# Attention inner loop on Trainium2: weighting V one key tile later, with three slots for the exponentials

## Chip, cores, metric

One Trainium2 chip, one program on all 8 of its cores. Each core takes one of the 8 batch elements (4096 tokens of width 1024) and does the whole computation for it; no data goes between cores. The metric is the device time in microseconds (us) of the slowest core.

## What is computed

For each batch element the reference does an attention block and a gated feed-forward block, each between two LayerNorms and with a residual. Cut to what matters:

```python
def attn(latents, gamma, beta, Wq, Wk, Wv, Wo):          # 16 heads of 64
    x = layernorm(latents) * gamma + beta
    q, k, v = x @ Wq, x @ Wk, x @ Wv                     # split into heads
    scores  = einsum('bhqd,bhkd->bhqk', q * s, k * s)    # s*s = 1/8
    weights = softmax(scores, axis=-1)
    return einsum('bhqk,bhkd->bhqd', weights, v) @ Wo
x = x + layernorm(attn(layernorm(x), ...))
x = x + layernorm(ffn(layernorm(x), ...))                # token shift, sigmoid gate, relu^2
```

## The kernel before

The kernel is written by hand, engine by engine. `ph.op(engine, ...)` (L34) puts an instruction at the end of one engine's list, `ph.wait` (L41) puts a wait on a semaphore there, and every engine works through its list in order. So what order things happen in is the order in which the Python code emits them, and the waits are those that are written out.

Stages: LayerNorm of the input and a bf16 copy to HBM; projections of Q, K and V (L356, L509); attention (L750 to L949) with the output projection and its LayerNorm for the query chunk before woven in; then the feed-forward stage (from L976). The change touches only the attention stage.

**Attention.** There are 8 chunks of 512 queries (`qc`), and in each 8 pairs of heads (`pj`), so 64 rounds (`idx`), here called heads' rounds, or rounds for short. A round goes over the 4096 keys in 32 key tiles of 128 (`kt`). One key tile is:

- *scores* (L782, TensorE): two matmuls, one for each head of the pair, 64 rows each, that run side by side on the array and write 128 keys x 512 queries each into `ps_sc`. `ps_sc` has four PSUM banks, so two key tiles' scores: the bank pair is `kt % 2`. Scores of tile `kt` wait for the exponential of `kt-2`, which empties that pair.
- *exponential* (L858, ScalarE): one ACTIVATE over both heads, 128x1024, from `ps_sc` to `exp_sb` in bf16. A fixed bound takes the place of the row maximum, so nothing is rescaled. `exp_sb` has two slots of 1024 columns, also by `kt % 2`.
- *weighting V* (L848, TensorE): two matmuls, one for each head, that add 65 x 512 into `ps_o[0]` and `ps_o[1]` over all key tiles. Row 65 comes from a column of ones in `v_sb` and is the sum of the exponentials.

TensorE's order is: scores of `kt`, then V of `kt-1`, which waits for the exponential of `kt-1`. The last tile's V matmuls (the *tail*, L871) are emitted in the next round, behind its first scores.

**End of a round.** VectorE waits for the tail (`s_mm2`), copies `ps_o` to `stage` (L885, two copies) and takes the reciprocal of the sums (L903, two of 1x512). The first V matmul of the next round waits for the two copies (`s_aev`), since it overwrites `ps_o`. In the next round, behind the scores of key tile 8, TensorE spreads the reciprocals over 64 rows (the *broadcast*, L914, four fp32 matmuls on `ps_bcj`, waiting for `s_rec`), VectorE multiplies (L923) into `attnb`, and the SyncE queue writes `attnb` to HBM (L930). In the last round of a chunk (`pj` = 7) ScalarE makes the reciprocals instead (L892, L897) and tail and broadcast stand at once at the end of the round.

**Woven in.** At key tile 8 of `pj` = 1, 3, 5 of every chunk but the first, TensorE also does 16 matmuls of the output projection (L629), between whose two halves it waits for a copy by VectorE (L637). ScalarE and VectorE do small LayerNorm steps at key tile 8 of the rounds.

Of the kernel before, what the change touches and what calls it, by code (L numbers as in the profile page):

```python
# [8 lines left out]
BF16 = mybir.dt.bfloat16  # L9
# [44 lines left out]
def build_nc(S=4096, D=1024, H=16, dh=64):  # L54
# [25 lines left out]
    with ExitStack() as top:  # L80
# [21 lines left out]
        d_attn = sem2("d_attn")  # L102
# [12 lines left out]
        s_exp = sem("s_exp")  # L115
        s_mm2 = sem("s_mm2")
# [11 lines left out]
        P = perm.enter_context  # L128
# [6 lines left out]
        stage_sb = [P(nc.sbuf_tensor(f"stage{i}", [128, 512], F32)) for i in range(4)]  # L135
        attnb_sb = [P(nc.sbuf_tensor(f"attnb{i}", [64, 512], BF16)) for i in range(4)]
        qm_sb = P(nc.sbuf_tensor("qm_sb", [1, 2 * NP * QC], F32))
# [17 lines left out]
        ph = Emit()  # L155
# [13 lines left out]
        Pc = p2core.enter_context  # L169
        kT_sb = Pc(nc.sbuf_tensor("kT_sb", [128, NP * S], BF16))  # L170
        exp_sb = Pc(nc.sbuf_tensor("exp_sb", [128, 2048], BF16))
        qtc_sb = Pc(nc.sbuf_tensor("qtc_sb", [128, NP * 512], BF16))
        ps_sc = Pc(nc.psum_tensor("ps_sc", [128, 2048], F32))
        ps_o = [Pc(nc.psum_tensor(f"ps_o{i}", [128, 512], F32)) for i in range(2)]
        ps_bcj = Pc(nc.psum_tensor("ps_bcj", [128, 512], F32))
        ps_bc = [ps_bcj[0:64, :], ps_bcj[64:128, :]]
# [67 lines left out]
        for i in range(NT):  # L244
# [31 lines left out]
            if i >= 2:  # L276
# [3 lines left out]
                  inc=s_s)  # L280
# [52 lines left out]
        for ch in range(QC):  # L333
# [14 lines left out]
            for (wsb, is_q) in ((wq_sb, True), (wk_sb, False)):  # L348
                for o in range(NP):
# [42 lines left out]
        for j2 in range(2 * NP):  # L392
# [15 lines left out]
              inc=s_v)  # L408
# [341 lines left out]
        for qc in range(QC):  # L750
# [8 lines left out]
            for pj in range(NP):  # L759
# [5 lines left out]
                for kt in range(KT):  # L765
# [25 lines left out]
                    if kt == min(8, KT - 1):  # L791
# [6 lines left out]
                        if qc >= 1:  # L798
# [23 lines left out]
                            else:  # L822
# [9 lines left out]
                                else:  # L832
# [4 lines left out]
                                    if pj < NP - 1:  # L837
                                        p3a_stepT(t0 + pj)
                    if kt >= 1:
                        if kt == 1 and idx >= 1:  # L840
                            ph.wait("tensor", s_aev, ps_o_free_chk[idx - 1])
                        ph.wait("tensor", s_exp, chk_kt[kt - 1])
                        bpo = ((kt - 1) % 2) * 2
                        for r2 in range(2):
                            hh = 2 * pj + r2
                            ph.op("tensor", lambda e, kt=kt, hh=hh, r2=r2, bpo=bpo,
                                  st=(kt == 1):
                                  e.matmul(ps_o[r2][0:65, :],  # L848
                                           v_sb[:, (kt - 1) * HW + hh * 65: (kt - 1) * HW + hh * 65 + 65],
                                           exp_sb[:, (bpo + r2) * 512:(bpo + r2 + 1) * 512],  # L850
                                           start=st, stop=False))
                    ph.wait("scalar", s_sct, sct_chk)
                    if kt == 0:
                        ph.wait("scalar", s_v, bias_ready)
                    if kt == 1 and idx >= 1:
                        ph.wait("scalar", s_mm2, 2 * idx)
                    ph.op("scalar", lambda e, bp=bp, pj=pj:
                          e.activation(exp_sb[:, bp * 512:(bp + 2) * 512],  # L858
                                       ps_sc[:, bp * 512:(bp + 2) * 512],
# [3 lines left out]

                def mk_tail(chk31=chk_kt[KT - 1], pj=pj):
                    def emit():
                        ph.wait("tensor", s_exp, chk31)
                        bpo = ((KT - 1) % 2) * 2
                        for r2 in range(2):
                            hh = 2 * pj + r2
                            ph.op("tensor", lambda e, hh=hh, r2=r2, bpo=bpo:  # L870
                                  e.matmul(ps_o[r2][0:65, :],  # L871
                                           v_sb[:, (KT - 1) * HW + hh * 65: (KT - 1) * HW + hh * 65 + 65],
                                           exp_sb[:, (bpo + r2) * 512:(bpo + r2 + 1) * 512],
                                           start=False, stop=True),
                                  inc=s_mm2)
                    return emit
# [55 lines left out]
                attn_w_chk[idx] = d_attn[pi].n
# [341 lines left out]
```

How the kernel before makes its waits and increments, by code:

```python
    def op(self, eng, fn, inc=None, k=1):  # L31
        if inc is not None:
            self.q[eng].append(lambda e, fn=fn, s=inc.h, k=k: fn(e).then_inc(s, k))
            inc.n += k
        else:
            self.q[eng].append(fn)
# [1 line left out]
    def wait(self, eng, sem, val=None):  # L38
        v = sem.n if val is None else val
        if v > 0:
            self.q[eng].append(lambda e, s=sem.h, v=v: e.wait_ge(s, v))
```

## Time and profile before

| what | us |
|---|---|
| median of 2 runs | 4059.81 (4054.91 to 4064.7) |
| the profiled execution, its own time | 4071.57 |
| span of its slowest core (core 2) | 4069.8 |
| spans of the eight cores | 4040.3 to 4069.8 |
| attention stage on core 2 (first exponential to last) | 691 to 3343 |

The profile shows one execution. The span goes from the first instruction to the last of a core. Instruction times are in us, or in ns where marked so. Idle time is put down to whatever released the engine. A pair of instructions of one line that overlap or touch is merged into one row of the timeline, with its count.

### The profile page before, as it was taken

How to read it: one execution, taken by the hardware profiler on the slowest of the kernel's cores; microseconds unless marked ns; L12 is line 12 of the kernel's file. 1: busy time of each engine (PE TensorE's matmuls, PEld its weight loads, DVE VectorE, ACT ScalarE, POOL GpSimd, SP SyncE). 2: the span in 40 equal slices, each digit the busy share in tenths (PEclk: the TensorE clock that was granted, in tenths of full speed). 3: DMA queues.
4: the chain of work that ended last, by engine and by line, in shares of the span. 5: the costliest groups of instructions: out<-in, count | busy, mean ns of one | idle time of the engine just before them, and what ended most of it. 6: DMA issues, size and time to landing. Idle time of an engine off the chain costs nothing.

```text
span 4069.8 us, 40105 instructions; the slowest of 8 cores (4040.3 to 4069.8 us)
## 1 busy us (share of the span) xinstructions
PE 2900.7 (71%) x12324; PEld 883.4 (22%) x12324; DVE 1411.9 (35%) x1953; ACT 2489.3 (61%) x2675; POOL 107.7 (3%) x201
## 2 busy tenths in 40 slices
PE   0477759777777777777778777777777772476675
PEld 0133323221222222222122222222212210232232
DVE  3466653212232232223233223322313223445444
ACT  3300001888888788788887878878888870232433
POOL 1011000000000000000000000000000001000000
PEclk9999979999999999999999999999999996777888
DMA  7521123000000100100101010010010005243241
GB/s 180 149 50 47 42 44 81 3 10 20 14 21 20 37 28 16 34 23 21 38 16 30 11 37 28 16 41 16 28 32 18 23 24 118 49 95 61 57 99 62
DMA packets 173284, 176.73 MB, mean 43 GB/s; under 512 B 112656, under 2 KB 137232, under 8 KB 173088
## 3 DMA queue, kind: packets, MB, share of 16 engines
q1 hardware_dynamic: 145792, 100.71, 10.5%
q0 software_dynamic: 22688, 65.07, 6.1%
q10 hardware_dynamic: 4608, 8.39, 0.6%
q8 instruction: 116, 1.90, 0.2%
q14 instruction: 80, 0.66, 0.1%
HBM read 96.49 MB, written 67.14 MB: 40 GB/s over the span
## 4 chain that ended last, share of the span: by engine, by line
PE 44%; ACT 31%; issue 9%; DVE 8%; DMA 3%; SPq 2%; DVEq 2%; ACTq 1%; POOL 0%; POOLq 0%
ACT exp_sb L858 28%; PE ps_o L848 15%; PE ps_sc L782 9%; PE ps_sc L356 6%; PE ps_sc L509 3%; PE ps_w L629 2%; PE ps_k L1130 2%; PE ps_wo L1104 2%; DVEq L44 2%; SPq L1045 2%; PE ps_bcj L914 2%; DVE sq_sb L311 1%; DMA wk_sb<-wk 1%; DVE xrT_sb L1076 1%; DVE xkT_sb L1082 1%
## 5 line engine op out<-in xcount | busy, mean ns | idle before, releaser
L858 ACT ACTIVATE exp_sb<-ps_sc,bias_cols 128x1024 bf16<-128x1024 f32 x2048 | 2181.6, 1111 | 580.5 <-PE ps_sc L782 579.1
L848 PE MATMUL ps_o<-exp_sb,v_sb 128*65 128x512 bf16 x3968 | 1198.3, 383 | 492.4 <-ACT exp_sb L858 414.3
L782 PE MATMUL ps_sc<-qtc_sb,kT_sb 64*128 64x512 bf16 x4096 | 808.6, 392 | 1.1 <-DVE v_sb L519 1.1
L885 DVE COPY stage<-ps_o 65x512 f32<-65x512 f32 x128 | 82.2, 681 | 1595.2 <-PE ps_o L871 1595.2
L848 PEld LDWEIGHTS ps_o<-exp_sb,v_sb 128*65 128x65 bf16 x3968 | 282.3, 109 | 1048.1 <-issue 1043.4
L782 PEld LDWEIGHTS ps_sc<-qtc_sb,kT_sb 64*128 64x128 bf16 x4096 | 196.0, 93 | 859.0 <-issue 859.0
L903 DVE RECIPROCAL stage<-stage 1x512 f32<-1x512 f32 x112 | 367.1, 3315 | 5.1
L1104 PE MATMUL ps_wo<-wrt_sb,xrT_sb 128*128 128x512 bf16 x512 | 138.9, 437 | 132.0 <-DVE xkT_sb L1085 80.9
L402 ACT ACTIVATE nmag_sb<-prod_sb 1x8 f32<-1x8 f32 x1 | 0.2, 207 | 369.9 <-DVE prod_sb L398 369.9
L1164 PE MATMUL ps_wo<-wvt_sb,kact_sb 128*128 128x512 bf16 x512 | 137.4, 433 | 111.2 <-DVE gg_sb L1185 98.3
L629 PE MATMUL ps_w<-wo_sb,at_sb 128*128 128x512 bf16 x512 | 141.2, 425 | 77.5 <-DVE wo_sb L637 67.4
L356 PE MATMUL ps_sc<-xat_sb,wq_sb 128*128 128x512 bf16 x512 | 121.8, 399 | 82.4 <-DMA xat_sb<-xa_h 82.4
L923 DVE TENSOR_TENSOR attnb<-stage,ps_bcj 64x512 bf16<-64x512 f32 x128 | 87.6, 684 | 192.9 <-PE ps_bcj L914 190.9
L356 PE MATMUL ps_sc<-xat_sb,wk_sb 128*128 128x512 bf16 x512 | 123.4, 403 | 0.0
L1130 PE MATMUL ps_k<-xkT_sb,wkt_sb 128*128 128x512 bf16 x512 | 119.1, 397 | 0.0
L509 PE MATMUL ps_sc<-wv_sb,xat_sb 128*128 128x512 bf16 x512 | 113.4, 385 | 4.3 <-DVE wv_sb L483 4.3
L1104 PEld LDWEIGHTS ps_wo<-wrt_sb,xrT_sb 128*128 128x128 bf16 x512 | 54.3, 109 | 216.9 <-issue 183.9
L1197 ACT ACT_TABLE_LOAD x8 | 10.3, 1283 | 148.4 <-DVE mv L1194 148.4
L914 PE MATMUL ps_bcj<-stage,ones128f 1*64 1x512 f32 x256 | 73.2, 648 | 33.2 <-ACT stage L897 33.2
L1164 PEld LDWEIGHTS ps_wo<-wvt_sb,kact_sb 128*128 128x128 bf16 x512 | 53.9, 108 | 194.8 <-issue 160.9
L1145 DVE TENSOR_TENSOR kact_sb<-k_sb 128x512 bf16<-128x512 bf16 x64 | 27.2, 426 | 185.8 <-ACT k_sb L1140 185.8
L629 PEld LDWEIGHTS ps_w<-wo_sb,at_sb 128*128 128x128 bf16 x512 | 49.6, 105 | 177.6 <-issue 140.5
(117 smaller groups left out, 1656.5 us busy)
## 6 DMA issues: line engine op xcount, KB each, us to landing
x_sb<-x SPq DMA_DIRECT2D x64, 512.0 KB, 5.1
x_h<-x1r_sb POOLq DMA_DIRECT2D x32, 512.0 KB, 2.9
x1c_sb<-x_h POOLq DMA_DIRECT2D x8, 2048.0 KB, 18.9
out<-ob_sb SPq DMA_DIRECT2D x8, 2048.0 KB, 12.6
xa_h<-xa_sb ACTq DMA_DIRECT2D x32, 256.0 KB, 4.7
qt_h<-qstage POOLq DMA_DIRECT2D x64, 128.0 KB, 2.2
qtc_sb<-qt_h SPq DMA_DIRECT2D x16, 512.0 KB, 4.8
attn_h<-attnb SPq DMA_DIRECT2D x128, 64.0 KB, 2.2
```

What stands on the lines that cost most here:

```text
L356: e.matmul(ps_sc[:, b * 512:(b + 1) * 512], w[:, c * D + o * 128: c * D + o * 128 + 128], xat_sb[:, (pxt * CT + c) * 512:(pxt * CT + c + 1 ...
L509: e.matmul(ps_sc[:, b * 512:(b + 1) * 512], xat_sb[:, (pxt * CT + c) * 512 + it * 128: (pxt * CT + c) * 512 + it * 128 + 128], wv_sb[:, c ...
L629: e.matmul(ps_w3[:], at3_sb[:, c * 512 + it * 128: c * 512 + it * 128 + 128], wo_sb[:, c * D + ec * 512: c * D + ec * 512 + 512], start=st ...
L782: e.matmul(ps_sc[:, (bp + r2) * 512:(bp + r2 + 1) * 512], kT_sb[lo:lo + 64, pj * S + kt * 128: pj * S + (kt + 1) * 128], qtc_sb[lo:lo + 64 ...
L848: e.matmul(ps_o[r2][0:65, :], v_sb[:, (kt - 1) * HW + hh * 65: (kt - 1) * HW + hh * 65 + 65], exp_sb[:, (bpo + r2) * 512:(bpo + r2 + 1) * ...
L858: e.activation(exp_sb[:, bp * 512:(bp + 2) * 512], ps_sc[:, bp * 512:(bp + 2) * 512], AF.Exp, bias=bias_cols[:, pj:pj + 1], scale=0.125),
L903: e.reciprocal(stage_sb[si][64:65, :], stage_sb[si][64:65, :]),
L914: e.matmul(ps_bc[r2], ones128f[64:65, :], stage_sb[si][64:65, :], start=True, stop=True, tile_position=(64, 64 * r2)), inc=s_bct)
L923: e.tensor_tensor(attnb_sb[si][:], stage_sb[si][0:64, :], ps_bc[r2], ALU.mult), inc=s_amu)
L1104: e.matmul(ps_wo[ppw][:, ec * 512:(ec + 1) * 512], xrT_sb[:, (pp * CT + c) * 512 + it * 128: (pp * CT + c) * 512 + it * 128 + 128], wrt_sb ...
L1130: e.matmul(ps_k3[ppk][:], wkt_sb[:, c * D + o * 128: c * D + o * 128 + 128], xkT_sb[:, (pp * CT + c) * 512:(pp * CT + c + 1) * 512], start ...
L1164: e.matmul(ps_wo[ppw][:, ec * 512:(ec + 1) * 512], kact_sb[:, c * 512 + it * 128: c * 512 + it * 128 + 128], wvt_sb[:, c * D + ec * 512: c ...
```

## The change

V is weighted two key tiles behind the scores, where it was one. Four things go with that. `exp_sb` gets a third slot, by `kt % 3`. The tail holds the V matmuls of the last two key tiles, 30 and 31. The first V matmul of a round, with its wait for VectorE's copies, now stands behind the scores of key tile 2, where it was tile 1. The first exponential of a round gets a wait of its own: for the V matmuls of key tile 30, which read the slot that it writes. `attnb` goes from four buffers to two, so the wait for its write to HBM moves from ahead of the copies to ahead of the multiply, and is for the write of one round before, where it was two.

```diff
-        attnb_sb = [P(nc.sbuf_tensor(f"attnb{i}", [64, 512], BF16)) for i in range(4)]
+        attnb_sb = [P(nc.sbuf_tensor(f"attnb{i}", [64, 512], BF16)) for i in range(2)]
...
-        exp_sb = Pc(nc.sbuf_tensor("exp_sb", [128, 2048], BF16))
+        exp_sb = Pc(nc.sbuf_tensor("exp_sb", [128, 3072], BF16))
...
-                    if kt >= 1:
-                        if kt == 1 and idx >= 1:
+                    if kt >= 2:
+                        ktg = kt - 2
+                        if kt == 2 and idx >= 1:
                             ph.wait("tensor", s_aev, ps_o_free_chk[idx - 1])
-                        ph.wait("tensor", s_exp, chk_kt[kt - 1])
-                        bpo = ((kt - 1) % 2) * 2
+                        eo = (ktg % 3) * 1024
...
                     if kt == 0:
                         ph.wait("scalar", s_v, bias_ready)
+                        if idx >= 1:
+                            ph.wait("scalar", s_mm2, 2 * idx - 1)
                     if kt == 1 and idx >= 1:
                         ph.wait("scalar", s_mm2, 2 * idx)
...
-                        ph.wait("tensor", s_exp, chk31)
...
+                        for ktg in (KT - 2, KT - 1):
+                            ph.wait("tensor", s_exp, chk30 if ktg == KT - 2 else chk31)
+                            eo = (ktg % 3) * 1024
...
+                                      inc=(s_mm2 if r2 == 1 else None))
...
-                if idx >= 2:
-                    ph.wait("vector", d_attn[pi], attn_w_chk[idx - 2])
...
                 ph.wait("vector", s_bct, 2 * (idx + 1))
+                if idx >= 1:
+                    ph.wait("vector", d_attn[(idx - 1) % 2], attn_w_chk[idx - 1])
```

**TensorE within a round.** The first rows of the attention stage. Before: scores of tiles 0 and 1 (L782), V of tile 0 (L848), scores of tile 2.

```order
L782 MATMUL ps_sc<-qtc_sb,kT_sb 128x512 [waits s_v,s_pjv,d_qtr0]
L782 MATMUL ps_sc<-qtc_sb,kT_sb 128x512 x3
L848 MATMUL ps_o<-exp_sb,v_sb 65x512 [waits s_exp]
L848 MATMUL ps_o<-exp_sb,v_sb 65x512
L782 MATMUL ps_sc<-qtc_sb,kT_sb 128x512 [waits s_exp]
L782 MATMUL ps_sc<-qtc_sb,kT_sb 128x512
```

After:

```order
L782 MATMUL ps_sc<-qtc_sb,kT_sb 128x512 [waits s_v,s_pjv,d_qtr0]
L782 MATMUL ps_sc<-qtc_sb,kT_sb 128x512 x3
L782 MATMUL ps_sc<-qtc_sb,kT_sb 128x512 [waits s_exp]
L782 MATMUL ps_sc<-qtc_sb,kT_sb 128x512
L848 MATMUL ps_o<-exp_sb,v_sb 65x512 x2
```

Scores of tile 2 now come ahead of V of tile 0, both need the same exponential, and the V matmuls have no wait of their own any more.

**TensorE across the end of a round.** From the last V matmuls inside round 0 to the fourth scores of round 1. L871 is the tail. Before:

```order
L782 MATMUL ps_sc<-qtc_sb,kT_sb 128x512 [waits s_exp,s_v]
L782 MATMUL ps_sc<-qtc_sb,kT_sb 128x512
L871 MATMUL ps_o<-exp_sb,v_sb 65x512 [waits s_exp]
L871 MATMUL ps_o<-exp_sb,v_sb 65x512
L782 MATMUL ps_sc<-qtc_sb,kT_sb 128x512 [waits s_exp]
L782 MATMUL ps_sc<-qtc_sb,kT_sb 128x512
L848 MATMUL ps_o<-exp_sb,v_sb 65x512 [waits s_aev,s_exp]
L848 MATMUL ps_o<-exp_sb,v_sb 65x512
```

After (the tail's line is now L875):

```order
L875 MATMUL ps_o<-exp_sb,v_sb 65x512 [waits s_exp]
L875 MATMUL ps_o<-exp_sb,v_sb 65x512
L875 MATMUL ps_o<-exp_sb,v_sb 65x512 [waits s_exp]
L875 MATMUL ps_o<-exp_sb,v_sb 65x512
L782 MATMUL ps_sc<-qtc_sb,kT_sb 128x512 [waits s_exp]
L782 MATMUL ps_sc<-qtc_sb,kT_sb 128x512
L782 MATMUL ps_sc<-qtc_sb,kT_sb 128x512 [waits s_exp]
L782 MATMUL ps_sc<-qtc_sb,kT_sb 128x512
L848 MATMUL ps_o<-exp_sb,v_sb 65x512 [waits s_aev]
L848 MATMUL ps_o<-exp_sb,v_sb 65x512
```

The tail has twice the matmuls, and one more pair of scores stands between it and the wait for the copies (`s_aev`).

**ScalarE at the start of a round with LayerNorm work** (L660, L663 are its small steps). Before:

```order
L858 ACTIVATE exp_sb<-ps_sc,bias_cols 128x1024 [waits s_sct,s_v]
L858 ACTIVATE exp_sb<-ps_sc,bias_cols 128x1024 [waits s_sct,s_mm2]
L858 ACTIVATE exp_sb<-ps_sc,bias_cols 128x1024 [waits s_sct] x6
L660 ACTIVATE rs_0<-mv_0,ceps_sb 128x1 [waits s_v]
L663 ACTIVATE rs_0<-rs_0 128x1
L858 ACTIVATE exp_sb<-ps_sc,bias_cols 128x1024 [waits s_sct] x24
```

After:

```order
L860 ACTIVATE exp_sb<-ps_sc,bias_cols 128x1024 [waits s_sct,s_v,s_mm2]
L860 ACTIVATE exp_sb<-ps_sc,bias_cols 128x1024 [waits s_sct,s_mm2]
L860 ACTIVATE exp_sb<-ps_sc,bias_cols 128x1024 [waits s_sct] x6
L660 ACTIVATE rs_0<-mv_0,ceps_sb 128x1 [waits s_v]
L663 ACTIVATE rs_0<-rs_0 128x1
```

The first exponential of a round has gained a wait for the tail's first half; all others stand as they stood.

## Rows read from the trace of the kernel before

**Rows 1.** The page: the granted TensorE clock in 40 slices, the chain by line.

```profile
PEclk9999979999999999999999999999999996777888
...
ACT exp_sb L858 28%; PE ps_o L848 15%; PE ps_sc L782 9%; PE ps_sc L356 6%; PE ps_sc L509 3%; PE ps_w L629 2%; PE ps_k L1130 2%; PE ps_wo L1104 2%; DVEq L44 2%; SPq L1045 2%; PE ps_bcj L914 2%; DVE sq_sb L311 1%; DMA wk_sb<-wk 1%; DVE xrT_sb L1076 1%; DVE xkT_sb L1082 1%
```

**Rows 2.** The page's groups: busy us, mean ns, idle before, releaser.

```profile
L858 ACT ACTIVATE exp_sb<-ps_sc,bias_cols 128x1024 bf16<-128x1024 f32 x2048 | 2181.6, 1111 | 580.5 <-PE ps_sc L782 579.1
```

**Rows 3.** Windows, attention stage: us, PE, PEld, DVE, ACT, POOL busy, PEclk, DMA, GB/s.

```profile
691.00:3343.00 2652.00, 2068.86 (x8884) 541.78 (x8884) 732.68 (x664) 2213.30 (x2184) 33.83 (x63) 0.98 0.08 23
```

**Rows 4.** Timeline inside a round: start, us, engine, line, count, idle before, releaser.

```profile
1157.08 2.12 ACT L858 ACTIVATE exp_sb<-ps_sc,bias_cols 128x1024 bf16<-128x1024 f32 x2 [0.15 <-PE ps_sc L782]
...
1158.34 0.59 PE L848 MATMUL ps_o<-exp_sb,v_sb 128*65 128x512 bf16 x2 [0.36 <-ACT exp_sb L858]
...
1158.87 0.39 PE L782 MATMUL ps_sc<-qtc_sb,kT_sb 64*128 64x512 bf16 x2
...
1159.36 2.12 ACT L858 ACTIVATE exp_sb<-ps_sc,bias_cols 128x1024 bf16<-128x1024 f32 x2 [0.16 <-PE ps_sc L782]
```

**Rows 5.** Timeline of TensorE just after projection work, when it catches up.

```profile
1142.94 0.39 PE L782 MATMUL ps_sc<-qtc_sb,kT_sb 64*128 64x512 bf16 x2
1143.26 0.62 PE L848 MATMUL ps_o<-exp_sb,v_sb 128*65 128x512 bf16 x2
1143.82 0.39 PE L782 MATMUL ps_sc<-qtc_sb,kT_sb 64*128 64x512 bf16 x2
```

**Rows 6.** Timeline at a chunk's start, where two tiles' scores lie ready.

```profile
1004.46 1.04 PE L782 MATMUL ps_sc<-qtc_sb,kT_sb 64*128 64x512 bf16 x4
...
1005.23 2.12 ACT L858 ACTIVATE exp_sb<-ps_sc,bias_cols 128x1024 bf16<-128x1024 f32 x2 [2.92 <-PE ps_sc L782]
```

**Rows 7.** Timeline across the end of a round.

```profile
1168.46 2.17 ACT L858 ACTIVATE exp_sb<-ps_sc,bias_cols 128x1024 bf16<-128x1024 f32 x2 [0.16 <-PE ps_sc L782]
...
1169.72 0.59 PE L871 MATMUL ps_o<-exp_sb,v_sb 128*65 128x512 bf16 x2 [0.36 <-ACT exp_sb L858]
...
1170.48 1.28 DVE L885 COPY stage<-ps_o 65x512 f32<-65x512 f32 x2 [25.27 <-PE ps_o L871]
1170.79 1.11 ACT L858 ACTIVATE exp_sb<-ps_sc,bias_cols 128x1024 bf16<-128x1024 f32 x1 [0.16 <-PE ps_sc L782]
...
1172.02 0.59 PE L848 MATMUL ps_o<-exp_sb,v_sb 128*65 128x512 bf16 x2 [1.39 <-ACT exp_sb L858]
...
1172.91 0.64 PE L848 MATMUL ps_o<-exp_sb,v_sb 128*65 128x512 bf16 x1
1173.08 1.11 ACT L858 ACTIVATE exp_sb<-ps_sc,bias_cols 128x1024 bf16<-128x1024 f32 x1 [1.18 <-PE ps_sc L782]
```

**Rows 8.** Timeline around the broadcast at key tile 8 of the same round.

```profile
1175.13 3.29 DVE L903 RECIPROCAL stage<-stage 1x512 f32<-1x512 f32 x1
...
1178.43 2.12 ACT L858 ACTIVATE exp_sb<-ps_sc,bias_cols 128x1024 bf16<-128x1024 f32 x2 [0.15 <-PE ps_sc L782]
...
1180.53 1.07 PE L914 MATMUL ps_bcj<-stage,ones128f 1*64 1x512 f32 x4
...
1180.91 1.10 ACT L858 ACTIVATE exp_sb<-ps_sc,bias_cols 128x1024 bf16<-128x1024 f32 x1
1181.53 0.62 PE L848 MATMUL ps_o<-exp_sb,v_sb 128*65 128x512 bf16 x2
...
1182.58 1.11 ACT L858 ACTIVATE exp_sb<-ps_sc,bias_cols 128x1024 bf16<-128x1024 f32 x1 [0.57 <-PE ps_sc L782]
```

**Rows 9.** Timeline of TensorE while its granted clock is half.

```profile
1009.53 1.06 PE L848 MATMUL ps_o<-exp_sb,v_sb 128*65 128x512 bf16 x2
...
1011.06 1.06 PE L848 MATMUL ps_o<-exp_sb,v_sb 128*65 128x512 bf16 x2
```

**Rows 10.** Windows: exp_sb's instructions alone (PE, PEld, ACT), then feed-forward, as rows 3.

```profile
1009.50:1012.00 2.50, 2.00 (x4) 0.37 (x4) 1.88 (x2) 0.50 0.84 275
...
3575.00:3610.00 35.00, 28.24 (x107) 11.33 (x105) 16.93 (x47) 6.84 (x10) 0.00 (x0) 0.81 0.57 105
```

More of the change, by code:

```diff
@@ L838, in build_nc @@
                                         p3a_stepT(t0 + pj)
-                    if kt >= 1:
-                        if kt == 1 and idx >= 1:
+                    if kt >= 2:
+                        ktg = kt - 2
+                        if kt == 2 and idx >= 1:
                             ph.wait("tensor", s_aev, ps_o_free_chk[idx - 1])
-                        ph.wait("tensor", s_exp, chk_kt[kt - 1])
-                        bpo = ((kt - 1) % 2) * 2
+                        eo = (ktg % 3) * 1024
                         for r2 in range(2):
                             hh = 2 * pj + r2
-                            ph.op("tensor", lambda e, kt=kt, hh=hh, r2=r2, bpo=bpo,
-                                  st=(kt == 1):
+                            ph.op("tensor", lambda e, ktg=ktg, hh=hh, r2=r2, eo=eo,
+                                  st=(kt == 2):
                                   e.matmul(ps_o[r2][0:65, :],
-                                           v_sb[:, (kt - 1) * HW + hh * 65: (kt - 1) * HW + hh * 65 + 65],
-                                           exp_sb[:, (bpo + r2) * 512:(bpo + r2 + 1) * 512],
+                                           v_sb[:, ktg * HW + hh * 65: ktg * HW + hh * 65 + 65],
+                                           exp_sb[:, eo + r2 * 512: eo + r2 * 512 + 512],
                                            start=st, stop=False))
@@ L854, in build_nc @@
                         ph.wait("scalar", s_v, bias_ready)
+                        if idx >= 1:
+                            ph.wait("scalar", s_mm2, 2 * idx - 1)
                     if kt == 1 and idx >= 1:
                         ph.wait("scalar", s_mm2, 2 * idx)
-                    ph.op("scalar", lambda e, bp=bp, pj=pj:
-                          e.activation(exp_sb[:, bp * 512:(bp + 2) * 512],
+                    ph.op("scalar", lambda e, bp=bp, pj=pj, eo=(kt % 3) * 1024:
+                          e.activation(exp_sb[:, eo:eo + 1024],
                                        ps_sc[:, bp * 512:(bp + 2) * 512],
@@ L862, in build_nc, with mk_tail @@
                     chk_kt[kt] = s_exp.n
-                def mk_tail(chk31=chk_kt[KT - 1], pj=pj):
+                def mk_tail(chk30=chk_kt[KT - 2], chk31=chk_kt[KT - 1], pj=pj):
                     def emit():
-                        ph.wait("tensor", s_exp, chk31)
[L867 to L875, printed above, removed]
+                        for ktg in (KT - 2, KT - 1):
+                            ph.wait("tensor", s_exp, chk30 if ktg == KT - 2 else chk31)
+                            eo = (ktg % 3) * 1024
+                            for r2 in range(2):
+                                hh = 2 * pj + r2
+                                ph.op("tensor", lambda e, ktg=ktg, hh=hh, r2=r2, eo=eo,
+                                      sp=(ktg == KT - 1):
+                                      e.matmul(ps_o[r2][0:65, :],
+                                               v_sb[:, ktg * HW + hh * 65: ktg * HW + hh * 65 + 65],
+                                               exp_sb[:, eo + r2 * 512: eo + r2 * 512 + 512],
+                                               start=False, stop=sp),
+                                      inc=(s_mm2 if r2 == 1 else None))
                     return emit
@@ L920, in build_nc @@
                 ph.wait("vector", s_bct, 2 * (idx + 1))
+                if idx >= 1:
+                    ph.wait("vector", d_attn[(idx - 1) % 2], attn_w_chk[idx - 1])
                 for r2 in range(2):
                     ph.op("vector", lambda e, si=pi * 2 + r2, r2=r2:
-                          e.tensor_tensor(attnb_sb[si][:], stage_sb[si][0:64, :], ps_bc[r2],
+                          e.tensor_tensor(attnb_sb[r2][:], stage_sb[si][0:64, :], ps_bc[r2],
                                           ALU.mult), inc=s_amu)
@@ L928, in build_nc @@
                     hg_ = 2 * pj + r2
-                    ph.op("sync", lambda e, si=pi * 2 + r2, hg_=hg_, qc=qc:
+                    ph.op("sync", lambda e, r2=r2, hg_=hg_, qc=qc:
                           e.dma_start(out=attn_hbm[hg_ * 64:(hg_ + 1) * 64, qc * 512:(qc + 1) * 512],
-                                      in_=attnb_sb[si][:]), inc=d_attn[pi], k=16)
+                                      in_=attnb_sb[r2][:]), inc=d_attn[pi], k=16)
                 attn_w_chk[idx] = d_attn[pi].n
```

## The prediction

> **What bounds the kernel now.** I read the page first. Its chain runs through the exponentials for 28% of the span, the V matmuls for 15% and the scores for 9% [rows 1]: two engines take turns on the path, so neither is the bound alone. The group of the exponentials says the same: 2048 of 1111 ns are busy for 2181.6 us, and ScalarE sat idle before them for 580.5 us, nearly all of it until scores came [rows 2]. The attention stage takes 2652 us, in which ScalarE is busy for 2213 and TensorE for 2069, at a granted clock of 0.98 [rows 3]. Neither is full. Something goes round in a circle.
>
> The timeline shows the circle [rows 4]. Exponentials come in pairs, 2.12 us long and 2.28 us apart (1157.08 to 1159.36). The first of a pair ends at 1157.08 + 1.11 = 1158.19. TensorE has waited for it, starts V at 1158.34 (0.15 later) and the next scores at 1158.87 (0.53 later), and the exponential of those starts at 1159.36 (0.49 later). So 1.11 + 0.15 + 0.53 + 0.49 = 2.28 us for two key tiles, 1.14 for one: the loop over a pair of score banks, with V matmuls standing in it between the exponential and the scores that refill its banks. That this is latency and not a full TensorE is seen in its 0.36 us of idle time ahead of V. (Over five pairs the mean is 1.137.)
>
> **Part 1: V leaves the loop.** The scores of tile k+2 still wait for the exponential of tile k, but no longer stand behind V. The loop over two tiles becomes 1.11 + 0.15 + 0.49 = 1.75 us, 0.88 for one. Two other limits then come in. ScalarE alone: where two tiles' scores lay ready, two exponentials took 2.12 us, so the second began 2.12 - 1.11 = 1.01 us behind the first [rows 6]. TensorE alone: catching up after the projection it did one tile's scores and V in 1143.82 - 1142.94 = 0.88 us [rows 5]. The largest of the three, 1.01, is ScalarE's, and it is what is late next. The gain is 1.137 - 1.012 = 0.125 us for each step from one exponential to the next. It holds for the steps into tiles 3 to 7 and 10 to 31, 27 in a round: 3.4 us, and 216 us over 64 rounds. What I have not seen is three exponentials in a row without a gap. Bounds for the steady step: 1.01 (row above) and 1.11 (no overlap at all, the mean duration of one [rows 2]). I take 1.01, since the overlap is there each time two stand together.
>
> The Trainium skill bears on this in "ScalarE: Activation LUTs", in what it says of the ACTIVATE instruction's timing: back-to-back ones overlap by about 93 ns, and one with a pointer bias costs about 280 ns plus 0.833 ns an element. By that page the step would be estimated at 280 + 853 - 93 = 1040 ns, and the gain at about 170 us in place of 216. The trace has 1.01 for the same thing, so that is used.
>
> **Part 2: the end of a round.** From exponential 31 of one round (1168.46) to exponential 2 of the next (1173.08) now go 4.62 us for three steps, because V of tile 0 waits for the two copies of 1.28 us and TensorE idles 1.39 us before it, with scores of tile 2 queued behind [rows 7]. After the change, counting from the start of exponential 31:
> - Exponential 30 started 1.01 earlier and ends at 0.10; scores of the new tile 0 start at 0.25, V of tile 30 at 0.57 (0.32 behind scores, as in [rows 5]) and its second matmul at 0.78, which ends 0.38 later. With a semaphore's 0.15 the new wait of exponential 0 ends at about 1.31, not 1.01: +0.30.
> - Exponentials 1 and 2 follow at 2.32 and 3.33. The tail still starts at 1.26 (1169.72 - 1168.46), the copies still end at 1171.76 - 1168.46 = 3.30 and V of tile 0 is released at about 3.5, as now (1172.02, 3.56). It now holds back the scores of tile 3: 3.56 + 0.53 + 0.49 = 4.58, where exponential 3 wanted 4.34, so up to +0.24; I take +0.17.
>
> That makes 3 x 1.01 + 0.30 + 0.17 = 3.50 for what took 4.62: 1.12 us saved in each of the 56 rounds' ends inside a chunk, 63 us. At the 8 chunk ends tail, copies and ScalarE's reciprocals stand in a row in both kernels: no change.
>
> **Part 3: the broadcast, the wait that comes in.** TensorE reaches it behind the scores of tile 8, in order, with V and the scores of tile 9 queued behind, and ScalarE waits for those. Now the second reciprocal ends at 1175.13 + 3.29 = 1178.42 and the broadcast starts at 1180.53: 2.1 us of cover [rows 8]. That cover goes. VectorE's chain is tied to the tail: 1178.42 + 0.15 is 8.85 us behind the tail's start, 10.11 in the count above. Exponential 6 ends at 1.31 + 6 x 1.01 + 0.17 + 1.11 = 8.65, scores of tile 8 start at 8.80, and the broadcast could start at 9.12. It waits 1.0 us. Then V comes 1.0 later (1181.53 - 1180.53), scores of tile 9 0.53 behind, its exponential 0.49 behind those: 12.13, where exponential 7 began at 8.55. So 3.58 for the two steps 7 to 9, against 1182.58 - 1179.44 = 3.14 now: 0.44 us lost in 56 rounds, 25 us. Without the wait it would be 2.6 (a gain of 30 us in place of a loss of 25), so the reciprocals' length costs 55.
>
> **Part 4: what costs nothing.** The projection work behind the broadcast has the same matmuls and the same wait for VectorE in both; nothing takes it off the path. ScalarE's LayerNorm steps at tile 8 fall into its wait for tile 9 as now. The wait for the write of `attnb` is for a DMA issued a whole round (over 30 us) earlier. VectorE is busy 733 of 2652 us [rows 3] and stays a bystander but for the reciprocals. If their cover or the DMA's were missing, the cost would be a wait at tile 8 of the kind priced above.
>
> **Sum.** 216 + 63 - 25 = 254 us. Against this, the gain of a step isn't had where the clock is at 1.2 GHz: there one tile takes 1011.06 - 1009.53 = 1.53 us in TensorE's own work [rows 9], with granted clock 0.50 [rows 10], before and after. A clock of 0.98 over 2652 us is 0.02 / 0.5 = 4% of the time at the low level, about 106 us or 70 tiles; I take off 14 us for these and for rougher joints at chunk starts. So 240 us: 4071.6 - 240 = 3832 for the profiled execution. The median of the runs shown stands 12 us below that execution, so I forecast 3820 us.
>
> **Rivals.**
> - *ScalarE can't keep up the overlap.* With 1.11 us a step, 216 falls to 27 x 64 x 0.027 = 47, and the other parts hardly move: 85 of gain remains less the same 14, about 3985. For it: no third exponential in a row in the trace. Against: no pair that stood ready took longer than 2.12. Halfway lies 3900.
> - *The wait moves and the clock with it.* After the idle 1.39 us of [rows 7] a V matmul took 0.64 in place of 0.38, so the clock had gone to 1.2 GHz. If the new waits at tile 8 do the same in every round for 3 or 4 tiles, each costs 1.53 - 1.01 = 0.52: 56 x 1.8 = 100 us, part of which before pays too. About 3880. Against: the longest idle piece gets shorter.
> - *The granted clock falls to 0.81.* The feed-forward stage of this core runs at 0.81 for stretches [rows 10], the attention stage never did. At 0.81 one tile takes TensorE up to 0.88 / 0.81 = 1.09 and it becomes the bound: 1728 steps x 0.08 = 138 us back, 3930 or a little more than that if the joints stretch too. The rows speak against it, since the denser projections of Q and K ran at 0.9 or more [rows 1].
> - *Slower than before.* TensorE is held at 1.2 GHz in most of the stage, because its work now comes in even, short pieces with a gap in each. A tile then costs 1.53, and with 0.52 lost for each tile the 3.8 us gained in a round are gone from 7 more tiles at the low clock in each, 11 us of some 35. At all tiles: 3820 + 2048 x 0.52 = 4885. Against: busy share rises, from 2069 of 2652 to 2069 of about 2410.
> - *It doesn't do what it says*: V without a wait would have to hold TensorE up in another way, such as scores that start late behind two V matmuls. The step would stay at 1.14 and only part 2 be left: about 4020.
>
> For the 0.81 case the Trainium skill has a rule that speaks against this change: "TensorE: Matmul & The Clock Gate", in the part on the HAM clock gate, says that a die goes to 13/16 of the clock once three of its cores run dense matmuls. By it the third rival would hold all through the attention stage, 3930. The trace agrees for the feed-forward stage (0.81) and not for the projections, so I give it little.
>
> **How the numbers follow.** Forecast 3820: 0.66. Clock falling after the new wait (3880): 0.12. ScalarE short of the overlap, halfway or wholly (3900 to 3985): 0.09. Clock at 0.81 (3930): 0.06. No effect on the step (4020): 0.04. Slower: 0.03. The range reaches down to 3765, where the broadcast's wait falls away (55 us) in a tighter round, and up to 3920, which takes in the second case and half of the third. A difference of 2% is 81 us, about what a measurement of this kernel can tell from no change. Faster by more: all cases under 3979, 0.92. Within 2%: the end of the third case and the fifth, 0.05. Slower 0.03.
>
> **What would show it.** Exponentials in an unbroken row 1.01 us apart in tiles 9 to 31; ScalarE's idle time before them down from 580 to some 340 us; the attention stage about 2410 us long; in each round a wait of TensorE for the second reciprocal ahead of the broadcast of about 1 us, and a step from tile 8 to 9 of 2.5 us; exponential 0 about 0.3 us late; granted clock at 0.97 or above. It is wrong if the steady step is over 1.03, if exponentials still come in pairs with 0.15 between, or if a clock of 0.5 or 0.81 stands in many windows of the stage.

## The result, and the profile after

The changed kernel takes 3841.46 us (median of 13 executions) against 4061.55 for the kernel before (median of 10): ratio 0.9452, 95% interval 0.9442 to 0.9462. That is 220 us less; the forecast was 240 less, 3820. In the execution that was profiled, die 1 ran at a lower granted clock (0.878 against 0.927) and took longer, so the rows below are those of core 2, on die 0 (span 3840.3 us); for the same reason the rows of one experiment are of another core, which is named.

The attention stage, as in [rows 3] (columns: us, PE, PEld, DVE, ACT, POOL busy, PEclk, DMA share, GB/s):

```profile
693.00:3121.00 2428.00, 2140.86 (x8879) 593.79 (x8876) 731.38 (x662) 2116.32 (x2184) 33.83 (x63) 0.96 0.09 26
```

It went from 2652 (2649 from first exponential to last) to 2428 us, which is all of the gain. And the granted clock fell from 0.98 to 0.96. ScalarE's busy time is smaller, though it does the same work, since exponentials now overlap throughout.

ScalarE over one round (timeline, core 2), the counterpart of [rows 4], [rows 7] and [rows 8] at once:

```profile
1124.17 1.22 ACT L860 ACTIVATE exp_sb<-ps_sc,bias_cols 128x1024 bf16<-128x1024 f32 x1
1125.79 8.15 ACT L860 ACTIVATE exp_sb<-ps_sc,bias_cols 128x1024 bf16<-128x1024 f32 x8 [0.39 <-PE ps_o L875]
...
1134.30 1.10 ACT L860 ACTIVATE exp_sb<-ps_sc,bias_cols 128x1024 bf16<-128x1024 f32 x1
1136.58 1.11 ACT L860 ACTIVATE exp_sb<-ps_sc,bias_cols 128x1024 bf16<-128x1024 f32 x1 [1.19 <-PE ps_sc L782]
1138.11 1.12 ACT L860 ACTIVATE exp_sb<-ps_sc,bias_cols 128x1024 bf16<-128x1024 f32 x1 [0.42 <-PE ps_sc L782]
1139.65 21.21 ACT L860 ACTIVATE exp_sb<-ps_sc,bias_cols 128x1024 bf16<-128x1024 f32 x21 [0.42 <-PE ps_sc L782]
```

Read it from the bottom. Twenty-one exponentials, tiles 11 to 31, stand in one unbroken row: from the end of the first (1.11 long) to the end of the last it is (21.21 - 1.11) / 20 = 1.005 us a step, where pairs with a gap of 0.15 stood before. The eight of tiles 0 to 7 likewise. What is left of the round are three places: exponential 0 comes 1125.79 - 1124.17 = 1.62 behind exponential 31, exponential 9 comes 2.28 behind exponential 8, and exponentials 10 and 11 each come 1.53 or 1.54 behind the one before, which is not 1.005.

The second and third, on TensorE and VectorE:

```profile
1127.62 6.55 DVE L905 RECIPROCAL stage<-stage 1x512 f32<-1x512 f32 x2
...
1134.42 1.07 PE L916 MATMUL ps_bcj<-stage,ones128f 1*64 1x512 f32 x4 [0.95 <-DVE stage L905]
1135.43 0.62 PE L848 MATMUL ps_o<-exp_sb,v_sb 128*65 128x512 bf16 x2
...
1135.98 0.50 PE L782 MATMUL ps_sc<-qtc_sb,kT_sb 64*128 64x512 bf16 x2
1136.41 1.06 PE L848 MATMUL ps_o<-exp_sb,v_sb 128*65 128x512 bf16 x2
```

TensorE idled 0.95 us before the broadcast until the second reciprocal was done. That is the new wait. The first pair of V matmuls behind it still takes 0.62 us, the second takes 1.06, as in [rows 9]: the clock has gone down. The windows of this round say so in one column:

```profile
1125.00:1136.00 11.00, 8.98 (x42) 2.42 (x40) 8.16 (x5) 9.93 (x12) 0.00 (x0) 1.00 0.00 0
1136.00:1139.50 3.50, 3.50 (x12) 0.68 (x11) 3.30 (x5) 2.23 (x2) 0.00 (x0) 0.52 0.15 37
1139.50:1161.00 21.50, 20.23 (x88) 5.66 (x87) 1.29 (x3) 21.21 (x21) 0.53 (x1) 1.00 0.14 50
```

Granted clock 1.00, then 0.52 for 3.5 us behind the broadcast, then 1.00. How often TensorE waited for the reciprocals, from the view of the broadcast's tile (idle time before it, us, times):

```profile
  DVE stage L905: 58.2, 56
```

58.2 / 56 = 1.04 us in every round inside a chunk. In the same view of the kernel before there is no such line.

The low clock, unlike the wait, doesn't come in every round. Here is an earlier broadcast, with a wait as long, and the 5 us from its start:

```profile
805.25 1.07 PE L916 MATMUL ps_bcj<-stage,ones128f 1*64 1x512 f32 x4 [1.06 <-DVE stage L905]
...
805.30:810.30 5.00, 4.94 (x22) 1.27 (x22) 1.37 (x2) 3.37 (x4) 0.00 (x0) 1.00 0.10 26
```

In such windows, one for each of the 56 waits on core 2, the granted clock is 0.54 to 0.77 in 31 and 1.00 in 25.

The chain of waits across that round, start, us, what, shows that this wait is no detail but part of the path:

```profile
1126.24 0.69 DVE stage L887
1126.93 0.60 DVEq L44
1127.62 6.57 DVE stage L905 x2
1134.42 1.07 PE ps_bcj L916 x4
1135.50 0.55 PE ps_o L848 x2
```

From the tail on, the path goes through VectorE's copies and reciprocals to the broadcast. Exponentials 0 to 8 aren't on it. Behind tile 11 the same view names TensorE's matmuls, and that is not to be read as TensorE setting the step. Where it catches up, the scores of two tiles start 0.87 us apart:

```profile
1140.05 0.39 PE L782 MATMUL ps_sc<-qtc_sb,kT_sb 64*128 64x512 bf16 x2
...
1140.92 0.39 PE L782 MATMUL ps_sc<-qtc_sb,kT_sb 64*128 64x512 bf16 x2
```

So TensorE could go faster than 1.005. That ScalarE sets the step is read from these rows; no run tested it apart.

### The profile page after: what moved, and what is told of

Read it like the earlier page. It is cut to its first block, busy times and chain, and to the rows that moved or that the text cites. A ratio compares the mean times of both kernels' runs of the same rounds, so it can differ in the third digit from the quotient of the medians.

```text
span 3933.1 us, 38249 instructions; the slowest of 8 cores (3818.4 to 3933.1 us)
## 1 busy us (share of the span) xinstructions
PE 3090.4 (79%) x12324; PEld 947.1 (24%) x12324; DVE 1414.1 (36%) x1953; ACT 2395.3 (61%) x2675; POOL 107.7 (3%) x201
## 4 chain that ended last, share of the span: by engine, by line
PE 61%; DVE 19%; issue 6%; ACT 4%; DMA 3%; DVEq 3%; SPq 2%; ACTq 1%; POOL 0%; POOLq 0%
PE ps_o L848 23%; PE ps_sc L782 15%; DVE stage L905 9%; PE ps_sc L356 7%; PE ps_sc L509 3%; PE ps_w L629 3%; DVEq L44 3%; PE ps_k L1134 2%; PE ps_bcj L916 2%; PE ps_o L875 2%; SPq L1049 2%; PE ps_wo L1108 2%; ACT exp_sb L860 1%; DVE sq_sb L311 1%; DMA wk_sb<-wk 1%
## 5 line engine op out<-in xcount | busy, mean ns | idle before, releaser
L860 ACT ACTIVATE exp_sb<-ps_sc,bias_cols 128x1024 bf16<-128x1024 f32 x2048 | 2087.5, 1153 | 483.3 <-PE ps_sc L782 453.7
L848 PE MATMUL ps_o<-exp_sb,v_sb 128*65 128x512 bf16 x3840 | 1257.2, 411 | 18.1 <-DVE stage L887 18.1
L782 PE MATMUL ps_sc<-qtc_sb,kT_sb 64*128 64x512 bf16 x4096 | 836.7, 400 | 119.1 <-ACT exp_sb L860 39.4
L782 PEld LDWEIGHTS ps_sc<-qtc_sb,kT_sb 64*128 64x128 bf16 x4096 | 234.1, 93 | 1066.1 <-issue 1066.1
L848 PEld LDWEIGHTS ps_o<-exp_sb,v_sb 128*65 128x65 bf16 x3840 | 277.8, 112 | 509.7 <-issue 505.9
L1108 PE MATMUL ps_wo<-wrt_sb,xrT_sb 128*128 128x512 bf16 x512 | 130.9, 418 | 129.9 <-DVE xkT_sb L1089 79.6
L629 PE MATMUL ps_w<-wo_sb,at_sb 128*128 128x512 bf16 x512 | 154.8, 457 | 74.5 <-DVE wo_sb L637 67.2
L356 PE MATMUL ps_sc<-xat_sb,wq_sb 128*128 128x512 bf16 x512 | 146.6, 458 | 83.8 <-DMA xat_sb<-xa_h 83.8
L356 PE MATMUL ps_sc<-xat_sb,wk_sb 128*128 128x512 bf16 x512 | 146.8, 459 | 0.0
L509 PE MATMUL ps_sc<-wv_sb,xat_sb 128*128 128x512 bf16 x512 | 135.0, 437 | 4.3 <-DVE wv_sb L483 4.3
L356 PEld LDWEIGHTS ps_sc<-xat_sb,wq_sb 128*128 128x128 bf16 x512 | 56.5, 113 | 177.6 <-issue 172.9
```

Of the source, the lines that this page charges most:

```text
L356: e.matmul(ps_sc[:, b * 512:(b + 1) * 512], w[:, c * D + o * 128: c * D + o * 128 + 128], xat_sb[:, (pxt * CT + c) * 512:(pxt * CT + c + 1 ...
L509: e.matmul(ps_sc[:, b * 512:(b + 1) * 512], xat_sb[:, (pxt * CT + c) * 512 + it * 128: (pxt * CT + c) * 512 + it * 128 + 128], wv_sb[:, c ...
L629: e.matmul(ps_w3[:], at3_sb[:, c * 512 + it * 128: c * 512 + it * 128 + 128], wo_sb[:, c * D + ec * 512: c * D + ec * 512 + 512], start=st ...
L782: e.matmul(ps_sc[:, (bp + r2) * 512:(bp + r2 + 1) * 512], kT_sb[lo:lo + 64, pj * S + kt * 128: pj * S + (kt + 1) * 128], qtc_sb[lo:lo + 64 ...
L848: e.matmul(ps_o[r2][0:65, :], v_sb[:, ktg * HW + hh * 65: ktg * HW + hh * 65 + 65], exp_sb[:, eo + r2 * 512: eo + r2 * 512 + 512], start=s ...
L860: e.activation(exp_sb[:, eo:eo + 1024], ps_sc[:, bp * 512:(bp + 2) * 512], AF.Exp, bias=bias_cols[:, pj:pj + 1], scale=0.125),
```

## The experiments

Ten kernels were run. The theory from the rows above was:

**Theory A.** Inside a round the step was set by the loop with V in it, and is now ScalarE's. In the changed kernel the chain tail, copies, reciprocals, broadcast sets when tile 9 comes; tiles 0 to 8 have slack beside it. So parts 2 and 3 of the prediction aren't two terms but one. And TensorE's idle time ahead of the broadcast brings the clock down behind it, which is the missing 20 us and more.

**Putting back the loop.** V one tile behind again. The first V matmuls of a round stay behind the scores of tile 2; the tail is one tile again, and with it goes the extra wait of exponential 0:

```diff
-                        eo = (ktg % 3) * 1024
+                        for ktg in ((0, 1) if kt == 2 else (kt - 1,)):
+                            if ktg == kt - 1:
+                                ph.wait("tensor", s_exp, chk_kt[kt - 1])
+                            eo = (ktg % 3) * 1024
...
-                        for ktg in (KT - 2, KT - 1):
+                        for ktg in (KT - 1,):
```

Expected: 

> The changed kernel with V one tile behind inside a round again (V of tiles 0 and 1 both behind the scores of tile 2, then scores of tile k, V of tile k-1), the tail of one tile, and the new joint of the rounds. Theory A (the step is set by the loop over the score banks with V in it): the step is back at 1.14 us from tile 10 on, 22 x 0.137 x 64 = 193 us more than the changed kernel, about 4030. Rival (most of the gain came from the joint of the rounds): about 3900.

Measured: 3997.66 us, ratio to before 0.9843 (0.9819 to 0.9867). The pairs are back:

```profile
1150.36 2.12 ACT L861 ACTIVATE exp_sb<-ps_sc,bias_cols 128x1024 bf16<-128x1024 f32 x2 [0.15 <-PE ps_sc L782]
...
1152.63 2.12 ACT L861 ACTIVATE exp_sb<-ps_sc,bias_cols 128x1024 bf16<-128x1024 f32 x2 [0.15 <-PE ps_sc L782]
```

2.27 us for two, as in [rows 4]. The loop explains the step: 156 us of the 220 come back with it, and what is left of the change, the new joint, is worth 66 (4064 to 3998). The figure of 193 us missed by some 37, since it was added to 3841. From exponential 9 to 31 of all 64 rounds, added up from the starts of the exponentials on core 2, this kernel takes 1601 us and the changed one 1433: 168 more. The changed kernel with a high clock behind the broadcast (the filler, below) takes 1405 there, and against that it is 196, as expected. So most of the 37 (196 - 168 = 28) is low clock in the changed kernel, which this one hardly has (its stage runs at 0.98); the rest lies ahead of exponential 9.

**The old joint in the changed kernel.** V of tile 0 ahead of the scores of tile 2 again:

```diff
+                    if kt == 2:
+                        if idx >= 1:
+                            ph.wait("tensor", s_aev, ps_o_free_chk[idx - 1])
+                        for r2 in range(2):
+                            ph.op("tensor", lambda e, hh=2 * pj + r2, r2=r2: e.matmul(ps_o[r2][0:65, :],
+                                  v_sb[:, hh * 65: hh * 65 + 65],
+                                  exp_sb[:, r2 * 512: r2 * 512 + 512], start=True, stop=False))
                     for r2 in range(2):
                         lo = r2 * 64
...
-                    if kt >= 2:
+                    if kt >= 3:
```

Expected: 

> The changed kernel, but V of key tile 0 with its wait for the two copies stands ahead of the scores of tile 2 again, where the kernel before had it; the rest as changed. Theory A (in the changed kernel tail, copies, reciprocals and broadcast are one chain that sets when tile 9 comes, so what happens to tiles 2 to 8 has slack): no change, 3841 plus at most 10 us, and the wait ahead of the broadcast shrinks by about 1 us. Theory B (the parts of the prediction add up): the 63 us of part 2 are lost, about 3900.

Measured: ratio to before 0.9368 (0.9328 to 0.9409), times 4064 is 3807; by the interval, 3791 to 3824. Undoing part of the change makes it *faster*, by some 34 us. Theory B is out (3900). Theory A was right that nothing is lost, and didn't see the gain. Core 6's stage, its joint and its broadcast:

```profile
691.00:3078.00 2387.00, 2083.80 (x8849) 586.18 (x8878) 731.58 (x662) 2113.97 (x2184) 33.84 (x63) 0.98 0.09 26
...
1154.61 0.59 PE L784 MATMUL ps_o<-exp_sb,v_sb 128*65 128x512 bf16 x2 [1.22 <-DVE stage L894]
...
1160.90 0.39 PE L791 MATMUL ps_sc<-qtc_sb,kT_sb 64*128 64x512 bf16 x2
1161.36 1.07 PE L923 MATMUL ps_bcj<-stage,ones128f 1*64 1x512 f32 x4
```

The wait moved from the broadcast back to the joint (1.22 us for the copies), the broadcast starts 0.46 behind the scores of tile 8 with no idle time for the reciprocals before it, and the stage runs at 0.98 where the changed kernel had 0.96. TensorE's busy time is 57 us less for the same matmuls (2083.80 against 2140.86), and in none of the 56 rounds is the clock low in the 5 us from the broadcast's start.

**The broadcast later.** One number:

```diff
-                    if kt == min(8, KT - 1):
+                    if kt == min(12, KT - 1):
```

Expected: 

> The changed kernel with the broadcast (and the projection work behind it) at key tile 12 in place of 8, one number changed. Theory A (the chain tail, copies, two reciprocals, broadcast sets the time to tile 9, and its wait also brings the clock down): the wait of about 1 us per round ahead of the broadcast goes, 70 to 100 us, and with it part of the time at a granted clock of 0.5 (now 365 us in the attention stage of core 2), another 40 to 70: 3690 to 3740 us. Theory B (the wait costs what the prediction said and the clock has other causes): 55 us less, 3786. Theory C (the wait is harmless): 3841.

Measured: 3737.24 us, ratio 0.9203 (0.9181 to 0.9226), 104 us under the changed kernel: in the range of theory A, outside B and C. The stage:

```profile
691.00:3008.00 2317.00, 2082.10 (x8874) 589.34 (x8875) 731.07 (x662) 2107.76 (x2184) 33.59 (x63) 0.99 0.09 27
```

Clock 0.99. Part of it is the wait itself (58 us by the row above); the rest, some 46 us, fits the clock, whose price the filler below measures alone. (The 365 us at a clock of 0.5 in this expectation and the next are too many: the changed kernel's stage at 0.96 makes it about 0.04 / 0.5 x 2428 = 194 us, an estimate from the window's row.)

Moved by one tile only (9 in place of 8), expected: 

> The changed kernel with the broadcast at key tile 9, one tile later. Theory A (the wait of 0.95 us ahead of the broadcast is all that is wrong with tile 8, and it is that idle time that the low clock follows): one tile of 1.0 us covers it, so the round falls by 0.9 us (50 us) and the stretches at a granted clock of 0.5 shrink from 365 to about 220 us in the attention stage (34 us): about 3755, near e1_bcast12. Rival (the broadcast needs several tiles of cover, or the clock has another cause): 3790 or more.

Measured: 3744.40 us, ratio 0.9219 (0.9197 to 0.9242). One tile is nearly all of it: the reciprocals were late by one tile and no more, and 3755 had been expected. A round of it, from the broadcast on:

```profile
1117.16 0.39 PE L782 MATMUL ps_sc<-qtc_sb,kT_sb 64*128 64x512 bf16 x2
1117.50 1.07 PE L916 MATMUL ps_bcj<-stage,ones128f 1*64 1x512 f32 x4
...
1118.38 23.39 ACT L860 ACTIVATE exp_sb<-ps_sc,bias_cols 128x1024 bf16<-128x1024 f32 x23
```

The broadcast follows the scores by 0.34 us, and 23 exponentials run without a gap behind it.

**The control.** The same edit, tile 12, in the kernel before. Expected: 

> The kernel before with the broadcast at tile 12. Theory A: there the reciprocals were done 2.1 us ahead of the broadcast, so moving it buys nothing: within 10 us of 4061. Rival (a later broadcast is good in itself): 50 us or more less.

Measured: 4062.15 us, ratio 1.001 (0.9982 to 1.0037). There the reciprocals had their 2.1 us of cover, and a later broadcast buys nothing.

**Both.** Broadcast at 12 and the old joint, to see whether the joint costs something once the slack beside it is gone. Expected: 

> Broadcast at tile 12 and V of tile 0 ahead of the scores of tile 2. Theory A: with the wait for the reciprocals gone the slack is gone too, and the old joint now costs its 1.0 us in each of the 56 rounds inside chunks, 55 us over e1_bcast12: about 3792. Rival (the joint costs nothing wherever the broadcast stands): 3737.

Measured: 3793.02 us, ratio 0.9343 (0.9327 to 0.9359), 56 us over the kernel with the broadcast at 12. That is the 55 that theory A expected. So the same edit, the joint, is worth 56 us with the reciprocals covered and less than nothing (-34) without.

**Is it the idle time that the low clock follows?** Four matmuls of which nothing is used, in the place of the wait:

```diff
-                        ph.wait("tensor", s_rec, rec_chk)
                         if idx >= 1:
                             ph.wait("tensor", s_amu, 2 * idx)
+                        if idx % NP != NP - 1:
+                            for _f in range(4):
+                                ph.op("tensor", lambda e, pj=pj: e.matmul(ps_bcj[:, :],
+                                      kT_sb[:, pj * S: pj * S + 128],
+                                      qtc_sb[:, pj * 512:(pj + 1) * 512], start=True, stop=True))
+                        ph.wait("tensor", s_rec, rec_chk)
```

Expected: 

> The changed kernel, broadcast at tile 8, with four matmuls of 128x512 whose result is thrown away (written to ps_bcj, then overwritten by the broadcast) ahead of the wait for the reciprocals: 0.86 us more work in each of 56 rounds, in the place of the idle time. Theory A (the low clock after the broadcast comes from TensorE's idle time there): the filler costs nothing, the stretches at 0.5 shrink to about 220 us, and the time falls to that of e2_joint_old, about 3807, though work was added. Rival (the clock is low there for another reason, the fp32 broadcast itself or the V and score matmuls behind it): 3841 or more.

Measured: 3787.99 us, ratio 0.9326 (0.9296 to 0.9355): 53 us less by doing 4 x 56 = 224 matmuls more (the trace keeps three of each four).

```profile
692.00:3068.00 2376.00, 2131.57 (x9041) 607.08 (x9105) 731.58 (x662) 2109.57 (x2184) 33.95 (x63) 0.99 0.09 26
...
1119.10 1.28 DVE L887 COPY stage<-ps_o 65x512 f32<-65x512 f32 x2 [22.31 <-PE ps_o L875]
...
1120.48 6.55 DVE L905 RECIPROCAL stage<-stage 1x512 f32<-1x512 f32 x2
...
1126.49 0.81 PE L916 MATMUL ps_bcj<-qtc_sb,kT_sb 128*128 128x512 bf16 x3 [0.16 <-issue]
1127.23 1.07 PE L923 MATMUL ps_bcj<-stage,ones128f 1*64 1x512 f32 x4
1128.23 0.62 PE L848 MATMUL ps_o<-exp_sb,v_sb 128*65 128x512 bf16 x2
...
1129.11 0.62 PE L848 MATMUL ps_o<-exp_sb,v_sb 128*65 128x512 bf16 x2
```

The broadcast still starts just behind the reciprocals (they end at 1120.48 + 6.55 = 1127.03, it starts at 1127.23), 8.13 us behind the start of the copies, where it was 1134.42 - 1126.24 = 8.18. But TensorE isn't idle ahead of it, V behind it takes 0.62, not 1.06, and the clock is 1.00 in the 5 us from the broadcast's start in all 56 rounds, where it was low in 31. The chain of VectorE is the same, so the 53 us are the clock's. 34 had been expected, from the run with the old joint; the intervals of the two ratios overlap, so the other 19 aren't shown to be a difference. The Trainium skill says in "TensorE: Matmul & The Clock Gate", in the part on the HAM clock gate, that the throttled state is the default and activity releases it; this pair of runs agrees, 0.96 without the filler and 0.99 with it.

**Four slots.** Room for a fourth slot of exponentials (by two buffers of `x1r` in place of three), so that ScalarE needs no wait for V:

```diff
-        exp_sb = Pc(nc.sbuf_tensor("exp_sb", [128, 3072], BF16))
+        exp_sb = Pc(nc.sbuf_tensor("exp_sb", [128, 4096], BF16))
...
-                        if idx >= 1:
-                            ph.wait("scalar", s_mm2, 2 * idx - 1)
-                    if kt == 1 and idx >= 1:
-                        ph.wait("scalar", s_mm2, 2 * idx)
```

Expected: 

> The changed kernel with four slots for the exponentials and neither wait of ScalarE for the V matmuls (two buffers in place of three for x1r make the room). Broadcast still at tile 8. Theory A: exponential 0 comes about 0.5 us earlier, but the chain from the tail sets tile 9, so no change: 3841 within 10. Rival (waits add up): 56 x 0.5 = 28 us less, 3813.

Measured in one execution, the profiled one (3847.3 us): core 2's stage 2428 us, the same as without it, at clock 0.96. The chain from the tail doesn't care when exponential 0 comes. With the broadcast at 12, expected: 

> Four slots and the broadcast at tile 12. Theory A: now the late exponential 0 is on the path and its 0.5 us per round is gained: 3737 - 28 = about 3709. Rival (exponential 0 is late for another reason, such as the scores of tile 0 behind two waits): 3737.

Measured, again in one execution (3728.7 us): stage 2309 us against 2317, spans up to 3727.0 against 3732.8. Some 8 us, not 28, so here theory A fell. The timeline has the reason:

```profile
1090.13 31.65 ACT L856 ACTIVATE exp_sb<-ps_sc,bias_cols 128x1024 bf16<-128x1024 f32 x31 [5.03 <-PE ps_sc L782]
...
1108.69 0.39 PE L782 MATMUL ps_sc<-qtc_sb,kT_sb 64*128 64x512 bf16 x2 [0.28 <-issue]
1109.01 1.06 PE L871 MATMUL ps_o<-exp_sb,v_sb 128*65 128x512 bf16 x4
1110.01 0.88 PE L782 MATMUL ps_sc<-qtc_sb,kT_sb 64*128 64x512 bf16 x4
1110.18 1.28 DVE L883 COPY stage<-ps_o 65x512 f32<-65x512 f32 x2 [18.28 <-PE ps_o L871]
...
1111.61 0.59 PE L848 MATMUL ps_o<-exp_sb,v_sb 128*65 128x512 bf16 x2 [0.72 <-DVE stage L883]
```

Exponential 0 is no longer late: the row of 31 runs through the joint without a gap. But the scores of tile 1 stand behind the tail of four matmuls, which follows the scores of tile 0 (1108.69) and ends at 1110.01, and those of tile 3 behind the wait for the copies. From exponential 0 to 8 it takes 8.5 us (median of the rounds), where it took 8.0 with three slots: the half microsecond is lost again there.

**The attnb part alone**, in the kernel before (two buffers, the wait ahead of the multiply). Expected: 

> The kernel before with two attnb buffers and the wait for their write ahead of the multiply, as in the change, nothing else. Both theories: no effect, within 5 us of 4061, since the awaited write is a round old. If the buffers mattered it would be slower, by up to one DMA landing of 2 us in each of 64 rounds, 4190.

Measured: 4064.29 us, ratio 1.0005 (0.9987 to 1.0022). No effect. Its use is room: the two buffers given up hold 2 x 512 bf16 values of a partition, as many as the third slot takes (1024). The change with attnb left alone was not run.

## Why the prediction was right, and where it was not

The parts, each as the time between starts of exponentials, added up over the rounds on core 2 (us; "gain" is before less changed):

| stretch | before | changed | gain | predicted | with filler |
|---|---|---|---|---|---|
| 31 to 2, 56 rounds (part 2) | 263 | 200 | 63 | 63 | 200 |
| 2 to 7, 56 rounds (part 1) | 322 | 280 | 42 | 35 | 281 |
| 7 to 9, 56 rounds (part 3) | 277 | 332 | -55 | -25 | 309 |
| 9 to 31, 64 rounds (part 1) | 1601 | 1433 | 168 | 176 | 1405 |
| up to 9 at the chunks' starts | 183 | 181 | 2 | 5 | 178 |

- *The bound (the loop with V in it).* Right. Taken out, the pairs go; put back, they return, 2.27 us for two.
- *Part 1, the step.* Right: 1.005 us against 1.01 taken, with bounds 1.01 and 1.11. The first rival (no sustained overlap) falls with the row of 21. The 1040 ns that the prediction estimated from the Trainium skill's "ScalarE: Activation LUTs", by what it says of the ACTIVATE instruction's timing, were 3.5% high; the measurement decides.
- *Part 2, the joint.* The size was right: 63 us in the stretch itself (and 66 for what remains of the change with the old loop, 56 with the broadcast at 12). Inside it two errors met: exponential 0 comes 1.62 behind exponential 31 (1.55 a round later), not 1.31, and tile 3 is not held up, where I had given it 0.17.
- *Part 3, the broadcast.* The wait is there in all 56 rounds, 1.04 us against 1.0. Its price was mis-sized: the steps from 7 to 9 lost 55 us, not 25, and 23 of that is low clock (with the filler it is 32). Taking the wait away gave 97 us (tile 9) to 104 (tile 12), where the prediction had 55.
- *The sum.* This is the step that was badly built. Parts 2 and 3 were worked out on one clock and then written as two terms. The gain of part 2 can't be had while the wait of part 3 exists: whatever tiles 0 to 8 gain, the broadcast's wait takes. Read as separate terms they would say that the old joint costs 63 us, and it costs nothing.
- *The allowance for the clock*, 14 us, is the other term that was mis-sized. I carried over the clock of the kernel before (0.98); it became 0.96, and by the filler that costs 53 us.
- *Luck.* With the clock high the stage gains 2647 - 2373 = 274 us, 20 more than the 254 of the sum, and the allowance was 39 too small. The two errors partly cancel, which is why 240 came within 20 of 220.
- *Signs.* ScalarE's idle time before exponentials is 457 us, not the 340 given as a sign: the rest of the gain shows as busy time (2213 to 2116), since overlapping exponentials count once. The clock of 0.96 is under the 0.97 that was asked for.
- *The second rival* had the mechanism, at a chance of 0.12 and with 3880, though not "in every round" but in 31 of 56. Its argument against (the longest idle piece gets shorter) didn't hold: 1.39 us at the joint became 0.95 ahead of the broadcast, and the clock got worse. So the likeliest case was part forecast, part second rival, and 3841 lies between 3820 and 3880.
- *The other rivals.* On core 2 the granted clock of the stage is 1.00 or 0.50 throughout, never 0.81; but on cores 4 to 7 of the same execution it was 0.81 for 467 to 582 us of the stage, so the third rival's level does occur there. (The 3930 of that rival doesn't follow from its own 138 us either: 3820 + 138 = 3958.) No effect and slower are out by the result.

Open is when the clock falls. The filler, and the broadcast at tile 9, where none of the 56 rounds has it either, show that it needs the idle piece ahead of the broadcast, but that piece isn't enough: 1.05 us of it are followed by low clock in 31 rounds and not in 25. In the kernel before, V of tile 0 waited over 1 us in 60 rounds, 1.39 in most, and the clock was low in the next 5 us in 16 of them. In the run with the old joint, 1.22 us at that place were followed by it in none. The places differ in what TensorE does around them (four one-row fp32 matmuls behind the one, V matmuls of all rows behind the other), and that wasn't taken apart.

## What to carry to other kernels

Where two engines are each busy for four fifths and neither is full, look for the loop over the buffers, add up its pieces from one turn, and take out of it whatever doesn't need to stand between the freeing of a buffer and its refilling. Before adding up what several edits gain, mark which of them lie on parallel branches of one chain: only the longest counts, and an edit on another is worth nothing, or its full price, depending on a third. A faster loop also eats the cover of everything placed by count of iterations (here a broadcast at tile 8), so such places have to be moved along: one number was worth about another 100 us here.

## What was not expected

- Idle time can be cheap or dear by its place: moving a wait of about 1 us from ahead of the broadcast to the joint raised the stage's granted clock from 0.96 to 0.98 and saved some 34 us.
- Useless work can save time: 4 matmuls in each of 56 rounds, in place of idle time, gave 53 us back.
- The exponential of 128x1024, alone 1.11 us long, goes at 1.005 us a step in rows of 21 and more. In such rows single ones are recorded longer (1.22 us for the last of one, the first row of the round above), so a mean duration (1111 ns in [rows 2]) is no guide to the rate.
